# A four-layer mixed model on one core: the 192 model columns as 128 and 64 instead of 96 and 96 in three stages

## What is computed

```
layer 0: relative-position attention (12 heads of 64), then 64 soft slots with their own MLPs
layer 1: gated convolution + attention (12 heads of 16), a = a + ...
         f = layernorm(a) * g3 + b3;  a = a + gelu(f @ ffn1_w + ffn1_b) @ ffn2_w + ffn2_b;  h = h + a
         then a top-2 router over 8 experts
layer 2: q, k, v = layernorm(h) @ w_q, @ w_k, @ w_v   (192 -> 768 each: 12 heads of 64)
         h = h + softmax(-like weights of q k^T / 8) v @ w_o + b_o
         h = h + gelu(layernorm(h) @ in_w + in_b) @ out_w
layer 3: decayed linear attention, then a top-2 router over 8 experts
```

## Time and profile before

| | us |
|---|---|
| median of 3 runs | 1642.98 |
| lowest and highest of them | 1640.08 and 1650.09 |
| profiled execution, its own time | 1650.37 |
| span of that profile, first to last instruction | 1648.6 |
| TensorE busy in it | 1402.0 (85%) |
| ScalarE, VectorE, POOL busy | 658.4, 676.0, 390.1 |
| mean granted TensorE clock, as a share of 2.4 GHz | 0.912 |

### The profile page before, as it was taken

The page is one execution under the profiler, slowest core; times in us unless marked ns, Lnnn a source line. Parts: engine busy times, 40 slices in busy tenths (PEclk is TensorE's granted clock), DMA queues, the critical chain, the costliest instruction groups (busy, mean ns, idle before and its releaser), DMA issues.

```text
span 1648.6 us, 31104 instructions
## 1 busy us (share of the span) xinstructions
PE 1402.0 (85%) x10060; PEld 1034.9 (63%) x10060; DVE 676.0 (41%) x2110; ACT 658.4 (40%) x2229; POOL 390.1 (24%) x473
## 2 busy tenths in 40 slices
PE   5898987678677778888998899699999999979994
PEld 3566555553233455666678799375676776779993
DVE  5557577611111765444325422344343323451113
ACT  1668566230001336777531122255554442213331
POOL 5213123220000222222101465121121100124441
PEclk8999798569886798999998999799999999989997
DMA  7433432629998000000005564200000300136553
GB/s 233 128 98 97 108 86 74 271 97 421 421 422 240 1 0 2 0 0 0 1 0 144 167 196 136 66 2 0 0 0 0 134 0 0 42 114 188 182 165 107
DMA packets 89958, 178.91 MB, mean 109 GB/s; under 512 B 35066, under 2 KB 53784, under 8 KB 88224
## 3 DMA queue, kind: packets, MB, share of 16 engines
q1 hardware_dynamic: 82720, 161.51, 29.6%
q0 software_dynamic: 7136, 16.10, 3.1%
HBM read 150.59 MB, written 27.18 MB: 108 GB/s over the span
## 4 chain that ended last, share of the span: by engine, by line
PE 53%; issue 17%; DVE 12%; SPq 8%; ACT 6%; DMA 3%; POOL 1%; DVEq 0%; POOLq 0%; ACTq 0%
PE bank L1835 13%; SPq L247 7%; PE bank L2351 6%; PE bank L2337 5%; PE bank L1926 4%; PE bank L1938 3%; PE bank L1955 3%; PE bank L2341 3%; PE bank L1965 3%; PE bank L2016 2%; PE bank L2008 2%; ACT ON L1623 2%; DVE MXU L934 1%; DMA SLOTS<-in_fc 1%; ACT PB L1623 1%
## 5 line engine op out<-in xcount | busy, mean ns | idle before, releaser
L1835 PE MATMUL bank<-XX,AREA 96*128 96x408 f32 (+1 forms) x640 | 240.7, 535 | 33.0 <-ACT XX L1577 15.7
L1835 PEld LDWEIGHTS bank<-XX,AREA 96*128 96x128 f32 (+1 forms) x640 | 122.7, 197 | 140.6 <-issue 101.5
L1926 PE MATMUL bank<-KZ,QT 128*102 128x102 f32 x1152 | 140.0, 261 | 8.8 <-ACT PB L1623 5.7
L673 POOL TENSOR_TENSOR PB<-PB,RCU 102x306 f32<-102x306 f32 x96 | 69.2, 720 | 328.1 <-DVE RCU L940 328.1
L657 POOL TENSOR_TENSOR RS<-VE,expo 102x4 f32<-102x4 f32 (+1 forms) x53 | 53.0, 1001 | 384.2 <-DVE VE L880 333.2
L1926 PEld LDWEIGHTS bank<-KZ,QT 128*102 128x102 f32 x1152 | 121.8, 174 | 26.6 <-issue 16.8
L2351 PE MATMUL bank<-WM,KZ 128*128 x660 | 118.2, 327 | 0.0
L2351 PEld LDWEIGHTS bank<-WM,KZ 128*128 128x128 f32 x660 | 105.7, 190 | 0.4
L1604 ACT ACTIVATE KZ<-bank,AREA 128x128 f32<-128x128 f32 x198 | 54.6, 375 | 122.1 <-PE bank L2341 119.2
L1938 PE MATMUL bank<-AREA,OT 128*102 128x192 f32 x384 | 90.2, 349 | 11.1 <-DVE SLOTS L1295 5.3
L1955 PE MATMUL bank<-PT,V 102*32 102x102 f32 (+1 forms) x1152 | 85.9, 270 | 15.9 <-DVE OT L950 13.7
(11 more groups left out here) (338 smaller groups left out, 2627.5 us busy)
## 6 DMA issues: line engine op xcount, KB each, us to landing
WM<-in_fc SPq DMA_DIRECT2D x10, 2304.0 KB, 21.0
AREA<-in_fc SPq DMA_DIRECT2D x8, 2304.0 KB, 21.8
SLOTS<-in_m3w SPq DMA_DIRECT2D x33, 384.0 KB
KZ<-in_fc SPq DMA_DIRECT2D x5, 2304.0 KB, 25.3
SLOTS<-in_m1w SPq DMA_DIRECT2D x33, 256.0 KB
AREA<-pos_scratch SPq DMA_DIRECT2D x16, 459.0 KB
pos_scratch<-AREA SPq DMA_DIRECT2D x8, 913.5 KB
pos_scratch<-SLOTS SPq DMA_DIRECT2D x8, 913.5 KB
```

Of the source, the lines that this page charges most:

```text
L673: pool.tensor_tensor(p, p, scale, ALU.mult).then_inc(sem["probs_ready"], 1)
L1835: last = pe.matmul(dst, lhsT, rhs, start=n == 0, stop=n == len(pieces) - 1)
L1926: last = pe.matmul(psum[k][0:T, cols(j)], QT[:, tile, cols(bb)], KALL[:, unit % per_tile * (HEADS // per_tile) + tile, cols(bb)], start=Tr ...
```

## The change

The three stages hold their 192 rows as 128 and 64, as the expert stages do.

- VectorE's `layernorm` gets an argument `twice`: four more tensor_scalar instructions a group write columns 128 to 192 twice over into XD (102 by 4 by 128), ahead of the four that write XN.
- `xw` turns XN's first 128 columns and XD instead of XN's two halves of 96; ScalarE's `turned_wide` copies both banks over 128 partitions to XW. The 64 rows then lie on partitions 0 to 63 and again on 64 to 127.
- `in_halves` takes batches of tiles in pairs (0, 3), (1, 4) and (2, 5). For a batch it first claims a bank for each tile, then issues one matmul of 128 rows for each tile, then the matmuls of 64 rows, pair by pair, the first of a pair on partitions 0 to 63 and the second on 64 to 127; each of these signals its bank.
- `mlp` takes the six tiles as a batch of four and a batch of two. The queries and keys go as three batches of four tiles on FBANKS, where they were single tiles on XBANKS. The values of a sequence claim both OBANKS, run two matmuls of 128 rows and then a pair of 64 rows.
- ScalarE reads the tiles in the new order (0, 3, 1, 4, 2, 5).
- The weights of these products are loaded in three transfers instead of one (`load_split`): layer 1 has ten more transfers, eight of them for the layernorm's scale and shift in the new layout with one number a partition, layer 2 has eight more.

```diff
@@ -82,8 +82,9 @@
-W1_LOADS = 6 + 8 + 8
-W2_LOADS = 8 + 6
+W1_LOADS = 6 + 8 + 8 + 2 + 8
+W2_LOADS = 8 + 6 + 4 * 2
+TILE_PAIRS = (((0, 3), (1, 4)), ((2, 5),))
@@ -186,6 +187,8 @@
+        XD = X1[:, :, 0:128]
+        XW = XX[:, 2 * GB * D:].rearrange("p (k t) -> p k t", k=2)
@@ -371,14 +374,15 @@
-        wf1, bf1, wf2, bf2 = a1(KD, 2, FF), a1(128, FT), a1(128, FT, D), a1(T, D)
+        wf1, bf1, wf2, bf2 = (a1(128, FF), a1(128, FF // 2)), a1(128, FT), a1(128, FT, D), a1(T, D)
+        g3, b3 = a1(128, 2), a1(128, 2)
...
-        wq2, wk2, wv2 = a2(KD, 2, FF), a2(KD, 2, FF), a2(KD, 2, FF)
+        wq2, wk2, wv2 = ((a2(128, FF), a2(128, FF // 2)) for _ in range(3))
...
-        wi2, bi2, wu2 = a2(KD, 2, FF), a2(128, FT), a2(128, FT, D)
+        wi2, bi2, wu2 = (a2(128, FF), a2(128, FF // 2)), a2(128, FT), a2(128, FT, D)
@@ -527,6 +531,11 @@
+            def load_split(w, src, name):
+                load(w[0], t[src][0:128], name)
+                for j in range(2):
+                    load(w[1][64 * j:64 * j + 64], t[src][128:D, j * (FF // 2):(j + 1) * (FF // 2)], name)
@@ -541,9 +550,16 @@
-                       (wf1, "ffn1", KD), (wf2, "ffn2", 128), (cw1, "conv1_w", 0), (cb1, "conv1_b", 0),
+                       (wf2, "ffn2", 128), (cw1, "conv1_w", 0), (cb1, "conv1_b", 0),
...
+            load_split(wf1, "ffn1", "w1_loaded")
+            for dst, src in ((g3, "ln_g"), (b3, "ln_b")):
+                v = t[src][:, 2, :]
+                for p0, p1, c, to in ((0, KD, 0, dst[0:KD, 0:1]), (0, 128 - KD, 1, dst[KD:128, 0:1]),
+                                      (128 - KD, KD, 1, dst[0:64, 1:2]), (128 - KD, KD, 1, dst[64:128, 1:2])):
+                    sp.dma_start(to, v[p0:p1, c:c + 1], allow_slow_non_contiguous=True
+                                 ).then_inc(sem["w1_loaded"], at.one("w1_loaded", 16))
@@ -595,8 +611,9 @@
-            load_area(((wq2, "q2", KD), (wk2, "k2", KD), (wv2, "v2", KD), (wo2, "o2", 128),
-                       (wi2, "in2", KD), (wu2, "up2", 128), (wqkv3, "qkv3", KD), (rt3, "router3", KD),
+            for w, src in ((wq2, "q2"), (wk2, "k2"), (wv2, "v2"), (wi2, "in2")):
+                load_split(w, src, "w2_loaded")
+            load_area(((wo2, "o2", 128), (wu2, "up2", 128), (wqkv3, "qkv3", KD), (rt3, "router3", KD),
@@ -873,7 +890,7 @@
-            def layernorm(src, dst, eps=EPS, name=None, stats=None):
+            def layernorm(src, dst, eps=EPS, name=None, stats=None, twice=None):
@@ -881,6 +898,10 @@
+                    if twice is not None:
+                        ts(twice[:, bb, :].rearrange("p (j k) -> p j k", j=2),
+                           src(bb)[:, 128:D].unsqueeze(1).to_broadcast([T, 2, D - 128]),
+                           MV[:, bb, 0:1], RS[:, bb:bb + 1], ALU.subtract, ALU.mult)
@@ -1295,7 +1316,7 @@
-                layernorm(a_of(g), xn, name="xn_ready")
+                layernorm(a_of(g), xn, name="xn_ready", twice=XD)
@@ -1304,6 +1325,9 @@
+            def prepare_f2(g):
+                layernorm(h_of(g), xn, name="xn_ready", twice=XD)
@@ -1494,7 +1518,7 @@
-                layernorm(h_of(g), xn, name="xn_ready")
+                layernorm(h_of(g), xn, name="xn_ready", twice=XD)
@@ -1521,11 +1545,11 @@
-            in_turns(prepare_a2, attend_2, lambda: prepare_h(0))
+            in_turns(prepare_a2, attend_2, lambda: prepare_f2(0))
...
-            in_turns(prepare_h, mlp_2, lambda: prepare_h(0))
+            in_turns(prepare_f2, mlp_2, lambda: prepare_h(0))
@@ -1577,11 +1601,22 @@
-            def hidden(tiles, func, bias, src_ready=None):
-                for m in range(tiles):
+            def turned_wide(scale=None, bias=None):
...
+                for part in range(2):
+                    k = at.bank(XBANKS)
+                    src = full(k)[:, 0:TG]
+                    if scale is None:
+                        free(activation(XW[:, part, :], src, ACT.Copy), k)
+                    else:
+                        free(activation(XW[:, part, :], src, ACT.Identity, scale=scale[:, part:part + 1],
+                                        bias=bias[:, part:part + 1]), k)
...
+            def hidden(func, bias):
+                for m in (m for batch in TILE_PAIRS for pair in batch for m in pair):
...
-                    free(activation(HT[:, m, :], src, func, bias=0.0 if bias is None else bias(m)), k)
+                    free(activation(HT[:, m, :], src, func, bias=bias(m)), k)
@@ -1764,8 +1799,8 @@
-                turned(XT, g1[:, 2, :], b1[:, 2, :])
-                hidden(FT, ACT.Gelu, lambda m: bf1[:, m:m + 1])
+                turned_wide(g3, b3)
+                hidden(ACT.Gelu, lambda m: bf1[:, m:m + 1])
@@ -1780,12 +1815,13 @@
-                turned(XT)
-                for p in range(6):
-                    k = at.bank(XBANKS)
+                turned_wide()
+                in_pairs = [m for batch in TILE_PAIRS for pair in batch for m in pair]
+                for p in in_pairs:
+                    k = at.bank(FBANKS)
...
-                for p in range(6):
-                    k = at.bank(XBANKS)
+                for p in in_pairs:
+                    k = at.bank(FBANKS)
@@ -1793,8 +1829,8 @@
-                turned(XT)
-                hidden(FT, ACT.Gelu, lambda m: bi2[:, m:m + 1])
+                turned_wide()
+                hidden(ACT.Gelu, lambda m: bi2[:, m:m + 1])
@@ -1885,13 +1921,39 @@
-            def mlp(tiles, w1, x, w2):
...
-                tokens = []
-                for m in range(tiles):
-                    k, p = claim(FBANKS)
-                    last = product(p[:, 0:TG], [(w1[:, part, m * 128:(m + 1) * 128], x(part)) for part in range(2)])
-                    tokens.append(filled(last, k))
+            def xw():
...
+                pe.wait_ge(sem["xn_ready"], at.take("xn_ready"))
+                turned = []
+                for src in (XN[:, :, 0:128], XD):
+                    k, p = claim(XBANKS)
+                    for bb in range(GB):
+                        last = pe.transpose(p[:, cols(bb)], src[:, bb, :], ident[0:T, 0:T])
+                    turned.append(filled(last, k))
+                fresh.append(True)
+                moved(*turned)
...
+            def in_halves(pairs_of, banks):
...
+                there = [[claim(banks) for _ in pair] for pair in pairs_of]
+                for pair, places in zip(pairs_of, there):
+                    for ((w, _), m), (k, p) in zip(pair, places):
+                        say_taken(pe.matmul(p[:, 0:TG], w[:, m * 128:(m + 1) * 128], XW[:, 0, :],
+                                            start=True, stop=False))
+                out = []
+                for pair, places in zip(pairs_of, there):
+                    for j, (((_, w), m), (k, p)) in enumerate(zip(pair, places)):
+                        rows, c = slice(64 * j, 64 * j + 64), m % 3 * 128
+                        out.append(filled(pe.matmul(p[:, 0:TG], w[rows, c:c + 128], XW[rows, 1, :],
+                                                    start=False, stop=True), k))
+                return out
...
+            def mlp(w1, w2, tiles=FT):
...
+                tokens = {}
+                for batch in TILE_PAIRS:
+                    done = in_halves([[(w1, m) for m in pair] for pair in batch], FBANKS)
+                    tokens.update(zip((m for pair in batch for m in pair), done))
@@ -2259,8 +2321,8 @@
-                xt()
-                mlp(FT, wf1, lambda part: XT[:, part, :], wf2)
+                xw()
+                mlp(wf1, wf2)
@@ -2376,24 +2438,27 @@
-                xt()
-                qk = []
-                for w in (wq2, wk2):
-                    for p6 in range(6):
-                        k, p = claim(XBANKS)
-                        qk.append(filled(product(p[:, 0:TG], two(w, p6 * 128, (p6 + 1) * 128)), k))
+                xw()
+                places = [[(w, m) for m in pair] for w in (wq2, wk2) for batch in TILE_PAIRS for pair in batch]
+                for first in range(0, len(places), 2):
+                    qk_moved = in_halves(places[first:first + 2], FBANKS)
...
-                    for c in range(0, FF, 2 * D):
-                        k, p = claim(OBANKS)
-                        v_moved.append(filled(product(p[0:T, 0:2 * D], token_rows(XT, bb, wv2, c, c + 2 * D)), k))
-                moved(*qk[-2:])
+                    there = [claim(OBANKS) for _ in range(2)]
+                    for j, (k, p) in enumerate(there):
+                        pe.matmul(p[0:T, 0:2 * D], XW[:, 0, cols(bb)], wv2[0][:, j * 2 * D:(j + 1) * 2 * D],
+                                  start=True, stop=False)
+                    for j, (k, p) in enumerate(there):
+                        rows = slice(64 * j, 64 * j + 64)
+                        v_moved.append(filled(pe.matmul(p[0:T, 0:2 * D], XW[rows, 1, cols(bb)], wv2[1][rows],
+                                                        start=False, stop=True), k))
+                moved(*qk_moved)
...
-                xt()
```

(3 more changed lines are left out.)

## The result

The changed kernel takes 1671.88 us (median of 4 runs, 1665.66 to 1683.88); the kernel before, measured beside it, 1645.01. The ratio is 1.0164, with a 95% interval of 1.0121 to 1.0207: 27 us slower. The prediction said 1652, within 1% of before, and its range ended at 1664.

What follows compares the result with a forecast made beforehand. TensorE's work was taken to set the pace, with PSUM copies hidden behind it. Third attention +14.6, layernorm +1.0 and closing products -6.8 made +8.8 us: 1652 against the median of 1643.0, range 1643 to 1664.

Steps and rivals of the forecast that it cites:

- The waits: Third attention: TensorE idles 1.14 and 2.16 us between query and key batches, 1.4 between value sequences, until copies free banks.
- the clock: Slower rival, chance 0.17: new idles in the third attention drop TensorE's clock once a group, +13.6 us, giving 1665.
- The pairs share the array, changes cost 0.2: New products: two 64-row passes together cost one pass, 0.342 us at 408 columns; changing row form costs 0.2 a batch.
- Queries and keys: Third attention: three batches of four tiles, 16.53 us as before up to 17.25; +0.3 a group taken.
- Values: Third attention: three sequences at 3.64 us and the last at 2.25, 13.17 against 10.32, +2.85 a group.
- Scores: Third attention: two copies stand before VectorE's first extremes, making the first exponentials 0.5 us late a group.
- transposes and `turned_wide`: no difference: Turned input: still eight transposes of 102 moving columns and two activations of 408, so no time change.
- Third attention without the clock: Sum of its waits and late scores: +3.65 us a group, +14.6 in four (8.4 to 17.6).
- Closing products: Second and third layers: -0.85 us a group, -6.8 in eight groups (-4.8 to -7.2); first half 7.41 against 8.32.
- Layernorm, transfers: VectorE's four added instructions cost 1.0 us once, ahead of the third attention; added transfers in layers 1 and 2 cost nothing.
- The rival without sharing: Slower rival, chance 0.03: 64-row passes go one by one, +6.7 us a group, +0.1 a closing group; +29, 1672.
- The first rival: Faster rival, chance 0.06: waits for banks do not hold in third attention and closing products; -29 us, 1614.

Runs made afterwards that it cites:

- the filled kernel: Against the changed kernel: useless unit-matrix matmuls put in TensorE's pauses in the third attention, no wait taken away; 1661.56 us, ratio 1.0107.
- pairs and four banks: Against the changed kernel: queries, keys and closing products in batches of two tiles, values rotating over four banks instead of two; 1630.87 us, ratio 0.9924.
- values one by one: Against the changed kernel: each bank of the values claimed alone and finished, 128 rows then 64, before the next; 1665.87 us, ratio 1.0133.
- four banks for the values alone: Against the changed kernel: only the value sequences of the third attention rotate over four banks instead of two; 1647.26 us, ratio 1.0045.
- old rows, new claims: Against the kernel before: rows still 96 and 96, only the change's order of claims in the third attention; 1673.39 us, ratio 1.0175.
- batches of one pair: Against the changed kernel: queries, keys and closing products in batches of two tiles, values as changed; 1649.52 us, ratio 1.0034.

## Why the prediction was wrong

The waits were read rightly, but the clock was put in the wrong case. Point by point:

- **The pairs share the array, changes cost 0.2**: right. A batch of four takes 4.48 (1135.66 to 1140.14), predicted 4.41; a sequence 2.29 (pauses gone), predicted 2.25.
- **The waits**: right in place and releaser. Predicted idles 1.14, 2.16 and 1.4; measured 1.21, 2.35 and 1.31 to 1.41. Queries and keys: +0.60 where the term was +0.3 (within its +0.7), since the first two batches' periods are 5.76 and 6.89 and not 5.55 and 6.57. Values: +3.11 where it was +2.85, a period of 3.7 and not 3.64 (within 3.75). Scores: +0.4 to 0.5, as predicted.
- **The start of the products**: a term that was missing. The idle before the first product is 1.03, not 0.69: +0.34 a group. The "transposes and `turned_wide`: no difference" failed by what stands behind them, where the new claims of four banks come; batches of two claims show 0.93.
- **Third attention without the clock**: +4.45 a group (67.24 to 67.30 in the filled kernel against 62.79), +17.2 in four with the first group's +3.8; predicted +14.6, upper bound 17.6.
- **Closing products**: -0.4 and -0.55 a group instead of -0.85, -3.8 instead of -6.8. The first half is 7.49 and not 7.31, and the second loses 0.18 and not 0.1. The start costs 0.21 more in the second layer and 0.07 in the third.
- **Layernorm, transfers**: at the head of the third attention 2.41 us from the first normalising row to the transposes (1046.36 to 1048.77) where it was 1.38, +1.03, predicted +1.0. POOL's copy ends at 532.24 and VectorE asks at 541.94, so 9.7 us of the 12.3 are left; the first expert's load starts 2.3 later (918.33 against 915.99), with a stage that begins 2.7 later. Both were hidden, as predicted.
- **The step that failed: the clock.** The rival had the right mechanism and 0.17 of the chance, because "no new idle is as long as 4.00" and "no row of before shows one after a pause this short". The first compared one pause with one pause, and the second holds for the rows that were shown, not for the trace. The rival's own price was off both ways: it had four falls at 3.4 us each; there were five, which cost 1.7 to 1.9 in queries and keys and 2.7 in the attention, 10.7 in all where it said 13.6. The prediction's own sign of being wrong, a window of the third attention below 1, came.

The trace of before has falls behind pauses as short as the new ones, in other stages. In the first layer's attention, and then in the router ahead of the first experts (its timeline, then windows with the columns of the earlier trace rows):

```profile
246.47 1.33 PE L2016 MATMUL bank<-AREA 64*102 64x203 f32 x8 [1.43 <-ACT AREA L1665]
...
906.45 1.14 PE L2299 MATMUL bank<-KZ,AREA 102*66 102x64 f32 x16 [1.23 <-issue]
...
913.59 2.07 PE L2299 MATMUL bank<-KZ,AREA 102*66 102x64 f32 x16 [1.23 <-DVE AREA L1403]
```

```profile
247.80:251.20 3.40, 3.40 (x19) 2.65 (x18) 1.12 (x3) 1.95 (x10) 0.69 (x1) 0.51 0.00 0
913.60:920.40 6.80, 6.49 (x39) 6.24 (x40) 4.51 (x20) 0.00 (x0) 2.04 (x2) 0.51 0.29 78
```

Behind a pause of 1.43 TensorE ran at 1.2 GHz for 3.4 us, behind four in a row of 1.21 to 1.23 (906.45 to 913.59) for 6.8. Against that stands the idle of 1.05 in the earlier trace rows, behind which the clock stayed at 1.00: such pauses bring a fall sometimes, which is a chance to be put on the rival and no reason to set it aside.

The balance: 1652 predicted; +2.6 for the waits of the third attention, +3.0 for the closing products, +10.7 for the clock make 1668; the median of before was 2.0 higher in these runs: 1670, measured 1671.9. The clock's 10.7 and the stages' terms are from one profile, the slowest of the four runs, so that the sum comes so near the median is in part luck. The granted clock was the largest single miss; without it the kernel takes 1661.56, within the range and still 1% slower, by its claims.

The rival without sharing gave 1672, the time that came, by a mechanism that did not happen: the pairs do share. (Its batch of 5.58 also leaves out the 0.2 for changing the row form that it would have to pay.) The first rival (waits that do not hold, 1614) is what the kernel with pairs and four banks comes towards at 1630.87: there the waits for banks are gone from queries, keys and values. The Trainium skill's rule on rotating through PSUM banks (page Perfetto Trace Analysis, Optimizing Tensor Performance) agrees with these runs: the same matmuls with two more banks for the values go from a ratio of 1.0164 to 1.0045. The Trainium skill's page TensorE: Matmul & The Clock Gate, A second HAM failure mode, which the prediction weighed and put aside for want of a row, tells of falls that come with frequent short pauses between groups of matmuls through banks. The traces agree for the queries and keys: falls in 11 of 12 groups with pauses of 1.21 and 2.35 us, and none behind the first group's head when the pauses are filled (ratio 1.0164 to 1.0107).

## What to carry to other kernels

A batch that fills all its banks at its end and is followed by a batch that claims all of them has no cover for its copies, however fast its matmuls are: claim by the smallest unit that shares the array (here a pair), and give the copying engine as many banks as TensorE claims. Where a change adds repeated pauses to a stage in which TensorE never paused, put a fall of the clock into the likeliest case, and look for falls and the pauses before them through the whole trace: here the changed stages had no such pauses, and others had falls behind pauses of 1.2 and 1.4 us. Filling the pauses with useless matmuls is a cheap test that tells waits from clock.

## What the runs showed of the hardware

- Behind pauses of 1.21 and 2.35 us in the queries and keys TensorE went from 2.4 to 1.2 GHz for 3.4 us, at a cost of 1.7 to 1.9: in three groups of four of the changed kernel, and in all four of each of the two runs that keep these pauses (values one by one, four banks for the values alone), 11 groups of 12. With pauses of 0.69 and 1.56 (old rows, new claims) it did so in one of four, with the pauses filled or gone in none.
- In the attention behind the values the link is weaker. Behind three pauses of 1.3 to 1.4 in the values it fell in two groups of four of the changed kernel (6.8 us, at a cost of 2.7) and in one of four with batches of one pair (3.4 us, at a cost of 1.2). With no pause in the values it fell in 2 groups of 12 (one with pairs and four banks, one with four banks for the values alone), and in none of the kernel before. What brings these falls was not settled.
- Changing between 128-row and 64-row passes costs some 0.175 each in passes of 384 columns that are not paired (0.82 for two passes against 0.645), which eats the gain of the 64 rows at once.
- Four claims of banks ahead of a stage's first product made TensorE start 0.10 to 0.11 later than two (idle 1.03 and 0.93 in the third attention, 1.40 and 1.29 and 0.90 and 0.79 in the closing products). Against one claim in the kernel before the difference is not constant: 0.34 in the third attention, 0.21 and 0.07 in the closing products. How the delay comes about was not tried.
